# The split parts of q and k in four slots, and q kept as three parts that are fetched with five transfers

## What is computed

```
qkv = x @ W_qkv.T + b_qkv              # q, k, v: (4, 16 heads, 1024, 8)
scores = q @ k.T / sqrt(8), causal     # (4, 16, 1024, 1024)
attn = softmax(scores);  O = attn @ v
x1 = layernorm(x + O @ W_o.T + b_o)
```

## Time and profile before

| | us |
|---|---|
| median of 3 runs | 861.2 (855.93 to 862.15) |
| profiled execution, its own time | 859.2 |
| its span, first to last instruction | 857.6 |
| first stage, to the end of its last weight copy | 61.4 |
| from there to the first scores of group 0 | 36.9 |
| TensorE, VectorE, ScalarE, GpSimd busy in the span | 739.3, 683.2, 567.2, 423.4 |
| data moved by DMA | 67.06 MB |

### The profile page before, as it was taken

The page is one execution under the profiler, slowest core; times in us unless marked ns, Lnnn a source line. Parts: engine busy times, 40 slices in busy tenths (PEclk is TensorE's granted clock), DMA queues, the critical chain, the costliest instruction groups (busy, mean ns, idle before and its releaser), DMA issues. The chain is left out here.

```text
span 857.6 us, 17568 instructions
## 1 busy us (share of the span) xinstructions
PE 739.3 (86%) x4345; PEld 323.0 (38%) x4345; DVE 683.2 (80%) x2289; ACT 567.2 (66%) x926; POOL 423.4 (49%) x468
## 2 busy tenths in 40 slices
PE   6758999999999999999999998696788888887755
PEld 4432233333332333233323331243456555554345
DVE  5669999898988898898889881156788888888883
ACT  4440267666766676667666767558889797897881
POOL 8655112221222112211222122267899999999984
PEclk9875699999999999999999999987999999999997
DMA  6757535335533653364336331201001101100000
GB/s 174 226 152 198 114 71 132 76 93 116 128 76 84 125 120 75 81 137 116 86 74 137 82 68 33 90 2 52 1 0 38 38 1 37 38 1 13 1 14 25
DMA packets 58955, 67.06 MB, mean 78 GB/s; under 512 B 15488, under 2 KB 33536, under 8 KB 58880
## 3 DMA queue, kind: packets, MB, share of 16 engines
q1 hardware_dynamic: 53120, 62.35, 30.5%
q10 hardware_dynamic: 5184, 2.36, 1.0%
q0 software_dynamic: 576, 1.57, 0.7%
HBM read 46.73 MB, written 19.53 MB: 77 GB/s over the span
## 5 line engine op out<-in xcount | busy, mean ns | idle before, releaser
L697 ACT ACTIVATE probs<-ps 128x384 f32<-128x384 f32 (+2 forms) x384 | 291.9, 810 | 174.4 <-PE ps L751 123.4
L668 POOL TENSOR_SCALAR_AFFINE_SELECT probs<-probs 128x256 f32<-128x256 f32 x256 | 102.9, 407 | 368.6 <-ACT probs L697 366.3
L807 DVE CUSTOM_DVE_ANT_0 junk<-ps,tri 128x256 bf16<-128x256 f32 (+3 forms) x512 | 229.1, 488 | 43.7 <-PE ps L719 36.0
L719 PE MATMUL ps<-Kx,Qx 128*128 128x512 bf16 (+3 forms) x768 | 230.8, 345 | 11.3 <-DVE mx L811 4.1
L751 PE MATMUL ps<-Qa,Ka 128*128 128x512 bf16 (+3 forms) x768 | 185.9, 328 | 15.0 <-DMA Qa<-m_scr 10.1
L737 PE MATMUL ps<-probs,Vg 128*9 128x512 f32 (+3 forms) x1536 | 159.3, 488 | 1.0 <-ACT Os L682 0.5
L811 DVE TENSOR_REDUCE mx<-ps 128x1 f32<-128x512 f32 x256 | 158.2, 679 | 0.3 <-DVE Vg L794 0.2
L719 PEld LDWEIGHTS ps<-Kx,Qx 128*128 128x128 bf16 x768 | 68.7, 97 | 204.4 <-DVE mx L807 124.8
L966 POOL TENSOR_TENSOR S<-sim 128x1024 f32<-128x1024 f32 x64 | 120.6, 1907 | 12.1 <-DVE A L1218 6.5
L1218 DVE SCALAR_TENSOR_TENSOR A<-S,T,ps 128x511 f32<-128x511 f32 x128 | 90.2, 741 | 11.3 <-ACT ps L1040 10.3
L751 PEld LDWEIGHTS ps<-Qa,Ka 128*128 128x128 bf16 x768 | 61.5, 97 | 90.8 <-ACT probs L697 44.3
(11 more groups left out here) (115 smaller groups left out, 868.5 us busy)
## 6 DMA issues: line engine op xcount, KB each, us to landing
Qx<-q_scr SPq DMA_DIRECT2D x48, 192.0 KB
Kx<-k_scr SPq DMA_DIRECT2D x48, 192.0 KB
Qa<-q_scr SPq DMA_DIRECT2D x48, 192.0 KB
Ka<-k_scr SPq DMA_DIRECT2D x48, 192.0 KB
o_scr<-Os SPq DMA_DIRECT2D x32, 256.0 KB, 2.1
q_scr<-qs SPq DMA_DIRECT2D x34, 128.0 KB, 3.3
k_scr<-qs SPq DMA_DIRECT2D x18, 128.0 KB, 3.3
xin<-in_L_attn_x_dram ACTq DMA_DIRECT2D x8, 256.0 KB, 3.7
```

Of the source, the lines that this page charges most:

```text
L668: pool.affine_select(out=diag, in_=diag, compare_op=ALU.is_ge, fill=0.0, base=0, pattern=[[0, 2], [1, P]], channel_multiplier=-1).then_inc ...
L697: act.activation(probs[:, k % 2, hh, 0:width], ps[:, bank:bank + 2, :].rearrange("p a c -> p (a c)")[:, 0:width], ACT.Exp, scale=SM_SCALE) ...
L719: pe.matmul(ps[:, X_BANK + f % X_SLOTS, 0:c1 - c0], Qx[:, u, hh, P * i:P * (i + 1)], Kx[:, u, hh, c0:c1], start=True, stop=True).then_inc( ...
L807: dve.tensor_tensor_reduce(out=junk[:, f % 4, 0:w], in0=src, in1=tri[:, CHUNK - w:CHUNK], scale=1.0, scalar=-BIG, op0=ALU.add, op1=ALU.max ...
```

## The change

`qs` gets four slots (`QS`), chunk n using slot n mod 4, with one pair of store semaphores for each slot; the engines wait for a slot's stores only from batch 2 on. The loops over the batches in the first stage are written out on all engines, and the waits on `p3_made` and `r_made` look two chunks back. `q_scr` has three places in place of five, so a chunk of q is stored in three transfers rather than five (with k, six in place of eight). In `load_parts` a rotated block of q is no longer one window: rotation 1 is fetched as parts 1 and 2 (16 partitions) and part 0 (8 partitions), rotation 2 as part 2 (8) and parts 0 and 1 (16). A load is then five transfers of q and three of k, eight in all (`LOADS`), for the same 1.18 MB. The order in SyncE's queue stays. The diff, cut to its core (the waits lose their offset `ONE` throughout):

```diff
--- before.py
+++ after.py
@@ -79,6 +79,8 @@
 FREE = 2
+QS = 4
+LOADS = 8
@@ -149,7 +151,7 @@
-    q_scr = nc.dram_tensor("q_scr", [GROUPS, GH, 5, DH, SEQ], BF16).ap()
+    q_scr = nc.dram_tensor("q_scr", [GROUPS, GH, PARTS, DH, SEQ], BF16).ap()
@@ -201,8 +203,8 @@
-        qk_stored = [sem(f"qk_stored{u}") for u in range(2)]
-        p3_stored = [sem(f"p3_stored{u}") for u in range(2)]
+        qk_stored = [sem(f"qk_stored{u}") for u in range(QS)]
+        p3_stored = [sem(f"p3_stored{u}") for u in range(QS)]
@@ -284,7 +286,7 @@
-        qs = operands.enter_context(nc.sbuf_tensor("qs", [P, 2, 2, PARTS, CHUNK], BF16))
+        qs = operands.enter_context(nc.sbuf_tensor("qs", [P, QS, 2, PARTS, CHUNK], BF16))
@@ -303,22 +305,25 @@
             for r in range(PARTS):
-                src = q_scr[g, :, r:r + PARTS, :, :].rearrange("n h s d t -> (n s d) h t")
-                eng.dma_start(qdst[rows * r:rows * (r + 1), :, :], src).then_inc(done, 16)
+                for at, parts in ((0, slice(r, PARTS)), (PARTS - r, slice(0, r))):
+                    if parts.stop > parts.start:
+                        n = DH * (parts.stop - parts.start)
+                        eng.dma_start(qdst[rows * r + DH * at:rows * r + DH * at + n, :, :], q_scr[g, :, parts, :, :].rearrange(
+                            "n h s d t -> (n s d) h t")).then_inc(done, 16)
                 eng.dma_start(kdst[rows * r:rows * (r + 1), :, :],
                               k_scr[g].rearrange("n h s d t -> (n s d) h t")).then_inc(done, 16)
 
-
-        STORES = 6
+        STORES = 4
...
         def store_parts(sp, b):
...
             for u in range(2):
 
                 sp.wait_ge(p2_made, 4 * b + 2 * u + 2)
-                for s in (0, 1, 3, 4):
-                    sp.dma_start(q_part(b, u, s), qs[:, u, 0, s % PARTS, :]).then_inc(qk_stored[u], 16)
                 for s in (0, 1):
-                    sp.dma_start(k_part(b, u, s), qs[:, u, 1, s, :]).then_inc(qk_stored[u], 16)
+                    sp.dma_start(q_part(b, u, s), qs[:, (2 * b + u) % QS, 0, s, :]).then_inc(
+                        qk_stored[(2 * b + u) % QS], 16)
+                    sp.dma_start(k_part(b, u, s), qs[:, (2 * b + u) % QS, 1, s, :]).then_inc(
+                        qk_stored[(2 * b + u) % QS], 16)
@@ -339,7 +344,7 @@
-                    for signal in (*qk_stored, v_ready, p3_made, s_ready, *o_stored, o_read):
+                    for signal in (s_ready, *o_stored, o_read):
@@ -360,11 +365,11 @@
-                    with sp.Fori(0, BATCH - 1) as b:
+                    for b in range(BATCH - 1):
                         store_parts(sp, b)
 
                     for u in range(2):
-                        sp.wait_ge(qk_stored[u], STORES * 16 + ONE)
+                        sp.wait_ge(qk_stored[u], STORES * 16)
@@ -384,26 +389,21 @@
-                    def third_parts(b, store=True):
+                    for b in range(BATCH):
                         for u in range(2):
-                            if not isinstance(b, int) or b > 0:
-
-                                pool.wait_ge(p3_stored[u], 32 * b)
+                            n = 2 * b + u
+                            if b > 1:
+                                pool.wait_ge(p3_stored[n % QS], 32)
                             for w in range(2):
-
-                                pool.wait_ge(p2_made, 4 * b + 2 * u + w + 1)
-                                pool.tensor_tensor(qs[:, u, w, 2, :], rf[:, u, w, :], qs[:, u, w, 1, :],
+                                pool.wait_ge(p2_made, 2 * n + w + 1)
+                                pool.tensor_tensor(qs[:, n % QS, w, 2, :], rf[:, u, w, :], qs[:, n % QS, w, 1, :],
                                                    ALU.subtract).then_inc(p3_made, 1)
-                            if not store:
-                                continue
-                            pool.wait_ge(p3_made, 4 * b + 2 * u + 2 + ONE)
-                            pool.dma_start(q_part(b, u, 2), qs[:, u, 0, 2, :]).then_inc(p3_stored[u], 16)
-                            pool.dma_start(k_part(b, u, 2), qs[:, u, 1, 2, :]).then_inc(p3_stored[u], 16)
-
-                    third_parts(0)
-                    with pool.Fori(1, BATCH - 1) as b:
-                        third_parts(b)
-                    third_parts(BATCH - 1, store=False)
+                            if b < BATCH - 1:
+                                pool.wait_ge(p3_made, 2 * n + 2)
+                                pool.dma_start(q_part(b, u, 2), qs[:, n % QS, 0, 2, :]).then_inc(
+                                    p3_stored[n % QS], 16)
+                                pool.dma_start(k_part(b, u, 2), qs[:, n % QS, 1, 2, :]).then_inc(
+                                    p3_stored[n % QS], 16)
 
@@ -427,29 +427,27 @@
-                    def first_parts(b, more):
+                    for b in range(BATCH):
                         for u in range(2):
-                            if more:
-
...
+                            n = 2 * b + u
+                            if b < BATCH - 1:
+
...
+                            if b > 1:
+                                act.wait_ge(qk_stored[n % QS], STORES * 16)
                             for w in range(2):
-                                act.wait_ge(qk_ready, 4 * b + 2 * u + w + 1)
+                                act.wait_ge(qk_ready, 2 * n + w + 1)
+                                if b > 0:
+                                    act.wait_ge(r_made, 2 * (n - 2) + w + 1)
                                 act.activation(qf[:, u, w, :], ps[:, 2 + 2 * w + u, :], ACT.Identity,
                                                bias=bqk[:, w:w + 1])
-                                act.activation(qs[:, u, w, 0, :], ps[:, 2 + 2 * w + u, :], ACT.Identity,
+                                act.activation(qs[:, n % QS, w, 0, :], ps[:, 2 + 2 * w + u, :], ACT.Identity,
                                                bias=bqk[:, w:w + 1]).then_inc(q_read, 1)
 
-                    with act.Fori(0, BATCH - 1) as b:
-                        first_parts(b, True)
-                    first_parts(BATCH - 1, False)
@@ -488,7 +486,7 @@
-                    with pe.Fori(0, BATCH - 1) as b:
+                    for b in range(BATCH - 1):
@@ -539,14 +537,15 @@
-                            dve.wait_ge(p3_made, 4 * b + ONE)
-                            dve.tensor_tensor(rf[:, u, w, :], qf[:, u, w, :], qs[:, u, w, 0, :],
+                            if b > 0:
+                                dve.wait_ge(p3_made, 2 * (n - 2) + w + 1)
+                            dve.tensor_tensor(rf[:, u, w, :], qf[:, u, w, :], qs[:, n % QS, w, 0, :],
                                               ALU.subtract).then_inc(r_made, 1)
                             dve.wait_ge(r_made, 2 * n + w + 1)
-                            dve.tensor_copy(qs[:, u, w, 1, :], rf[:, u, w, :]).then_inc(p2_made, 1)
-                        dve.wait_ge(v_ready, n + 1 + ONE)
+                            dve.tensor_copy(qs[:, n % QS, w, 1, :], rf[:, u, w, :]).then_inc(p2_made, 1)
@@ -596,15 +595,19 @@
                     for u in range(2):
-                        sp.wait_ge(p3_made, 4 * (BATCH - 1) + 2 * u + 2 + ONE)
-                        sp.dma_start(q_part(BATCH - 1, u, 2), qs[:, u, 0, 2, :]).then_inc(qk_stored[u], 16)
-                        sp.dma_start(k_part(BATCH - 1, u, 2), qs[:, u, 1, 2, :]).then_inc(qk_stored[u], 16)
+                        sp.wait_ge(p3_made, 4 * (BATCH - 1) + 2 * u + 2)
+                        sp.dma_start(q_part(BATCH - 1, u, 2), qs[:, (2 * BATCH - 2 + u) % QS, 0, 2, :]).then_inc(
+                            qk_stored[(2 * BATCH - 2 + u) % QS], 16)
+                        sp.dma_start(k_part(BATCH - 1, u, 2), qs[:, (2 * BATCH - 2 + u) % QS, 1, 2, :]).then_inc(
...
+                            qk_stored[(2 * BATCH - 2 + u) % QS], 16)
...
                     for u in range(2):
-                        sp.wait_ge(qk_stored[u], STORES * 16 * BATCH + 32 + ONE)
-                        sp.wait_ge(p3_stored[u], 32 * (BATCH - 1))
+                        for slot, stores in ((u, 2 * STORES), (u + 2, 2 * STORES + 2)):
+                            sp.wait_ge(qk_stored[slot], 16 * stores)
+                        sp.wait_ge(p3_stored[u], 64)
+                        sp.wait_ge(p3_stored[u + 2], 32)
@@ -742,7 +745,7 @@
-                            pe.wait_ge(sop_loaded[u], 6 * 16 * load)
+                            pe.wait_ge(sop_loaded[u], LOADS * 16 * load)
...
```

More of the change, by code:

```diff
@@ L428, in _ @@
                     act.sem_inc(q_read, 2 * FREE)
-                    def first_parts(b, more):
+                    for b in range(BATCH):
                         for u in range(2):
-                            if more:
[L434 to L440, removed]
-                                           xT[:, u, :], ACT.Identity, bias=bo_col[:, 0:1]).then_inc(xb_made, 1)
-                            act.wait_ge(qk_stored[u], STORES * 16 * b + ONE)
```

(31 more changed lines are left out.)

## The result

The changed kernel takes 926.5 us (median of 5 runs, 914.17 to 931.28), against 860.9 for the kernel before on the same chip: a ratio of 1.072, with an interval of 1.068 to 1.076. The ratio leaves out the run of 931.28 us, which was a slow one. The forecast said 901, with 846 to 932. The profiled execution took 914.2 us (span 912.4), 55.0 more than the 859.2 of the one before. It is at the low end of the runs.

What follows compares the result with a forecast made beforehand. It took store waits to hold up the first stage, and the `m_scr` store queued behind loads to set attention turns 0 to 12. From 859.2 us, -8 (first stage) + 44 (loads) + 6 (clock) gave 901, range 846 to 932.

Steps and rivals of the forecast that it cites:

- The chain that decides: Attention turns 0 to 12: the `m_scr` store waits behind loads, so each us of longer load lengthens the span by one.
- The price of the pieces: Split `q` transfers in the attention loads: +3.4 us a turn, 13 turns, +44 us; bounds 0 to +5.2 a turn.
- the same upper end of +68: Attention loads under the port rule: pieces of four and two ports take as long as the six-port whole, +68 us.
- Transfers as such: Attention loads: eight issues take 3.5 us where six took 2.6, free while the load drains longer than it is issued.
- The clock: Turn starts: a longer TensorE idle gap brings half speed, 0.5 us a turn, +6 us; bounds 0 and 22.
- The first stage: Up to the last weight copy: four slots remove store waits, -10.6 us; the longer first load shrinks the gain to -8.
- The 2 us for the cut: First `Qx` load, end of first stage: split transfers lengthen it by 2 us, landing at 53.5 instead of 51.5.
- the 8.9 for a load of whole transfers: First `Qx` load: taken to last 8.9 us from its first issue, as in an attention turn (133.12 to 142).
- The sum: Whole kernel: 859.2 - 8 + 44 + 6 = 901 us, made against the profiled execution.
- the loads keep their length: Rival, attention loads: split transfers are no slower per byte, only the first stage moves, 849 us; chance 0.20.
- The serial case: Rival, attention turns: pieces fully serial and clock falls each turn, 13 x (5.2 + 1.7) = 90, 941 us; chance 0.13.

Runs made afterwards that it cites:

- The single loads: Kernel before with q transfers cut into 16 and 8 partitions in one load only: `Qa` alone 910.1 us, `Qx` alone 890.8 us.
- the exchanged order: Changed kernel with the row maxima sent to `m_scr` and fetched back before the `Qx`/`Kx` load starts: 881.9 us, ratio 1.024.
- strided pieces: Kernel before with rotated q blocks cut into pieces of every second partition (two of 12), 858.9 us, or every third (three of 8), 889.9 us.
- 12 + 12: Kernel before with each rotated q block fetched in two contiguous pieces of 12 partitions: 880.1 us, ratio 1.022.
- 16 + 8: Kernel before with rotated q blocks fetched in pieces of 16 and 8 partitions in both loads, all else kept: 933.8 us, ratio 1.081.
- the cut along heads: Kernel before with each rotated q block fetched in two pieces of all 24 partitions by two heads: 860.1 us, ratio 0.997.
- the first stage alone: Changed kernel's first stage, but five places in `q_scr` and six whole transfers a load, against the kernel before: 852.0 us, ratio 0.987.
- 8 + 8 + 8: Kernel before with each rotated q block fetched in three contiguous pieces of 8 partitions: 921.8 us, ratio 1.071.

## Why the prediction was right, and where its sizes were off

*The chain that decides* was right. Two loads stand ahead of the `m_scr` store, what lengthens either lengthens the turn, and it does so in all of turns 0 to 12. The single loads (+48 and +29) and the exchanged order show it. Because this wait was found under a TensorE that is busy 96% of the time, the sign came out right.

*The price of the pieces*, +3.4 us a turn, was too low: the stall rose by 4.0 us a turn, within the bounds of 0 and 5.2. The reason given was "by how few partitions it spreads over". The runs sharpen it: as far as they go, it is how close together the partitions lie. Twelve partitions over a stretch of 24 cost nothing, twelve in a row do. The rule of the Trainium skill ("SBUF — State Buffer", Door 1: The DMA port swizzle) says just this, that bandwidth goes by how many ports the partitions reach; strided pieces reach all six ports of the whole, and this case agrees in kind. It does not agree in size: by the rule, with the pieces one after another, 12 + 12 would cost as much as 16 + 8 and bring the same upper end of +68, and the runs have +18 and +72.

*Transfers as such*: costed at nothing, and 860.1 us for the cut along heads shows it.

*The clock*, +6, was about 12. The stall at a turn's start grew past 5 us and the half speed came at 11 turns of 12, where 0.5 us a turn was taken. The median run seems to have lost more to it than the profiled one: it is 12.3 us longer, at a mean granted clock of 0.908 against 0.923. That is 30 us more at half speed (an estimate: 2 x 0.092 x 924.8 less 2 x 0.077 x 912.4), worth up to 15 us if TensorE was busy in them; no trace shows that.

*The first stage*: -10.6 was forecast to the end of the last weight copy, -12.9 measured. 0.8 us of the difference is the pace: VectorE took 4.35 us a chunk and not 4.6, as ScalarE's rows show, so ScalarE's last chunk starts at 41.61 and not at 42.4.

```profile
28.56 0.69 ACT L446 ACTIVATE qf<-ps,bqk 128x512 f32<-128x512 f32 x1 [0.51 <-PE ps L480]
...
32.91 0.69 ACT L446 ACTIVATE qf<-ps,bqk 128x512 f32<-128x512 f32 x1 [0.51 <-PE ps L480]
```

The other 1.5 us are in the chain behind that chunk, which the prediction carried over as unchanged. It was 8.3 us long (53.02 to 61.36) and is 6.9 (41.61 to 48.49). Before, TensorE came to the weights after 5.5 us of idleness, at a granted clock of 0.51; now it comes to them after 0.86 us, at 1.00 (from 41.6 to 50 us), and the same two matmuls take 0.46 us in place of 0.77:

```profile
44.14 0.46 PE L502 MATMUL ps<-center,wo_nat 128*128 128x128 f32 x2 [0.86 <-issue]
```

But TensorE starts only 6.0 us earlier, not 8, as the first load took 14.1 us and not 10.9. The 2 us for the cut were right; the 8.9 for a load of whole transfers, taken from a turn of the attention, are 12.1 here. (The 8.9 were read from issue to next issue; the DMA share is 0.10 from 141.5 to 142 us, so the load's data end some 0.6 us sooner.) Windows of the kernel with the first stage alone:

```profile
42.40:46.00 3.60, 1.96 (x16) 1.56 (x15) 3.53 (x9) 2.81 (x6) 2.14 (x2) 1.00 0.82 227
46.00:50.00 4.00, 1.16 (x8) 0.97 (x8) 2.05 (x7) 0.60 (x1) 2.16 (x4) 0.87 0.80 140
```

Up to 46 us 227 GB/s move, more than the 151 of a load by itself: the last stores, issued up to 42.2 us, still move beside it. Behind them the load goes at nearly its rate of the attention. What of the 3.2 us are the stores ahead, and what the next load, whose issue starts at 49.33, no run separates.

*The sum*: -8 + 44 + 6 = +42 forecast, -6 + 48 + 12 = +54 measured. Each term missed to the same side, and the time still fell within the range. These sums are made against the profiled execution, 914.2 us; the median, 926.5, lies another 12 us above. Of the rivals, "the loads keep their length" gave 849; it is what the kernel with the first stage alone does, 852.0. It fell on its one condition, the pieces. The serial case (5.2 us a turn and the clock at every turn, 941) is nearer to the median than the forecast is, for all its chance of 0.13; to the profiled execution it is not. I had weakened the term from 5.2 to 3.4 by judgement between bounds. The step that failed is that one, and with it the clock, which follows from the gap.

## What to carry to other kernels

- Don't cut a transfer to a few neighbouring partitions. If it must be cut, cut it along the free dimension (heads here), or so that each piece still spans the stretch of the whole; and look at what the strided form costs the issuing queue (0.84 us in place of 0.30).
- On a shared queue, look for the small transfer that somebody waits for behind the bulk. Its time from issue to landing (6.9 us for 24 KB, 1.5 without a load ahead) tells how much each longer load will cost, long before an engine looks idle.
- A change of two parts should be taken apart: the first stage alone gives 852.0 us, 1.3% faster than before, and the new way of loading buries it under 74 us.

## What was not expected of the hardware

- Moving bulk transfers behind a small one brought a stall of VectorE of up to 3.8 us, with the longer loads up to 6.5 us, at the start of every second turn, with "issue" as its cause and packets on an instruction queue beside it. In the kernel before the profile puts every wait of VectorE between 98 and 520 us down to TensorE, those of 1.8 to 2.3 us at the same six places too, so how much of the stall is new stays open.
- 16 + 8 partitions are slower than 8 + 8 + 8 (933.8 against 921.8 us), although there are fewer and wider pieces, and much slower than 12 + 12 (880.1). Unequal pieces cost something that neither their number nor their compactness explains. The DMA engines are also busy longer for each MB (93 us against 80). A strided 16 + 8 was not tried; what it is stays open.
- A load of whole transfers, 8.9 us in the attention, takes 12.1 at the end of the first stage, from its first issue to TensorE's start.
